# A graph network on one core: the second layer's gathers of sampled rows, without their wait for the mean matmuls of two groups back

## The reference, cut to what matters

```python
def _sage_mean(h, src, dst, W_self, W_neigh, b):
    agg = jax.ops.segment_sum(h[src], dst, num_segments=N_NODES)
    deg = jax.ops.segment_sum(jnp.ones((src.shape[0],), h.dtype), dst, num_segments=N_NODES)
    mean_neigh = agg / jnp.maximum(deg, 1.0)[:, None]
    return h @ W_self + mean_neigh @ W_neigh + b
h = relu(_sage_mean(x, src, dst, W_self0, W_neigh0, b0))
h = _sage_mean(h, src, dst, W_self1, W_neigh1, b1)
x = layernorm(x + h)
...
kj = k[src] + e                      # e = edge_attr @ We + be
alpha = einsum('ehd,ehd->eh', q[dst], kj) / sqrt(D)
attn = softmax of alpha over the edges of one dst
out = segment_sum((v[src] + e) * attn) + (x @ Wskip + bskip)
x = layernorm(x + elu(layernorm(out) @ Wlin + blin + x))
```

## Time and profile before

| | us |
|---|---|
| three runs | 1755.62, 1757.79, 1760.14 |
| median | 1757.79 |
| the profiled execution, own time | 1751.26 |
| its span, first to last instruction | 1749.4 |

### The profile page before, as it was taken

One profiled execution on the slowest core, in us unless ns is written; L12 is line 12 of the kernel. 1 busy time (PEld: TensorE's weight loads), 2 busy tenths in 40 slices (PEclk: granted clock), 3 DMA queues, 4 the chain that ended last, 5 costly groups with the idle time before them and its releaser, 6 DMA issues. The chain is left out here.

```text
span 1749.4 us, 34139 instructions
## 1 busy us (share of the span) xinstructions
PE 1524.3 (87%) x7745; PEld 1024.5 (59%) x7745; DVE 1327.1 (76%) x6197; ACT 1160.0 (66%) x3125; POOL 1041.2 (60%) x1038
## 2 busy tenths in 40 slices
PE   3599999999999998999688867999999999999872
PEld 2477777777777776777455543555555555455441
DVE  4799999999999996656366653777777777777762
ACT  0499999999999995333255541666666666666662
POOL 4688888868888773664455526455555555555320
PEclk9899999999999999999899988999999999999995
DMA  2356566544444442332388853233222232333210
GB/s 79 109 152 158 153 160 154 151 154 144 149 142 148 139 146 74 85 84 70 116 268 271 273 173 80 78 84 85 83 84 84 84 85 79 82 83 85 59 36 4
DMA packets 178820, 206.77 MB, mean 118 GB/s; under 512 B 36607, under 2 KB 104666, under 8 KB 178703
## 3 DMA queue, kind: packets, MB, share of 16 engines
q1 hardware_dynamic: 151502, 169.25, 31.5%
q0 software_dynamic: 27200, 36.26, 9.0%
HBM read 107.47 MB, written 106.49 MB: 122 GB/s over the span
## 5 line engine op out<-in xcount | busy, mean ns | idle before, releaser
L1307 POOL DMA_INDIRECT big<-x_tab,look x196 | 199.6, 1019 | 97.6 <-issue 56.1
L1324 POOL DMA_INDIRECT out_dram<-big,idx x98 | 99.2, 1013 | 259.1 <-DVE big L1640 126.3
L700 PE MATMUL pb<-MG_s,big 128*128 128x256 f32 x832 | 207.4, 392 | 41.5 <-issue 30.7
L700 PEld LDWEIGHTS pb<-MG_s,big 128*128 128x128 f32 x832 | 149.5, 189 | 143.7 <-issue 95.2
L725 ACT ACTIVATE big<-big 128x128 f32<-128x128 f32 x416 | 170.0, 481 | 0.0
L820 POOL TENSOR_TENSOR big<-big,cl 128x512 f32<-128x512 f32 x104 | 133.3, 1282 | 49.8 <-ACT big L749 40.5
L682 PE MATMUL pb<-C_s,big 128*128 128x128 f32 x832 | 161.6, 276 | 0.0
L683 PE MATMUL pb<-Ws1c_s,big 128*128 128x128 f32 x832 | 161.3, 276 | 0.0
L1057 POOL DMA_INDIRECT big<-h1e_tab,hidx x98 | 97.9, 999 | 103.9 <-PE pb L937 45.0
L334 POOL DMA_INDIRECT a_xs<-in_x_dram,idx x98 | 102.3, 1044 | 86.7 <-issue 47.6
L1408 PEld LDWEIGHTS pb<-Wg_s,big 128*128 128x128 f32 x784 | 95.8, 192 | 98.1 <-ACT big L1480 95.8
(11 more groups left out here) (345 smaller groups left out, 4015.1 us busy)
## 6 DMA issues: line engine op xcount, KB each, us to landing
big<-in_x_dram SPq DMA_DIRECT2D x104, 256.0 KB
x_tab<-big SPq DMA_DIRECT2D x98, 256.0 KB
out_dram<-big SPq DMA_DIRECT2D x98, 256.0 KB
ve_tab<-c_ve SPq DMA_DIRECT2D x98, 256.0 KB
c_ve<-ve_tab SPq DMA_DIRECT2D x98, 256.0 KB
h1e_tab<-a_rows SPq DMA_DIRECT2D x25, 256.0 KB
x_tab<-a_rows SPq DMA_DIRECT2D x25, 256.0 KB
big<-eT_tab SPq DMA_DIRECT2D x98, 64.0 KB
```

The lines of the kernel that those rows point to most:

```text
L700: t = pe.matmul(o, b_x1T[:, r * P:(r + 1) * P], MG_s[:], start=True, stop=True)
L1307: g.indirect_dma_start(out=o, out_offset=None, in_=x1_tab, in_offset=bass.IndirectOffsetOnAxis(ap=look[:, a, j:j + 1], axis=0), bounds_che ...
```

## The change

One line of `c_pool` is removed: POOL no longer waits for the mean matmuls of group `s - 2` before it issues the gathers of group `s`. The wait for the gathers of group `s - 4` stays, and so does PE's wait for the gathers of its group. No other engine's instructions change; the lines after L1054 have numbers lower by one.

```diff
         def c_pool(g):
             for s in range(NG):
                 landed_before(g, dma_c[s % 4], R * (s // 4))
-                after(g, "c_pmT", s - 2)
                 for r in range(min(R, NT - R * s)):
                     t = R * s + r
                     g.indirect_dma_start(out=h1s[:, t, :], out_offset=None, in_=h1e_tab,
```

## The result

The changed kernel takes 1864.01 us (median of 4 runs, 1863.36 to 1865.36), the kernel before 1756.84 (4 runs beside it, 1755.62 to 1760.14). The ratio is 1.0608, with a 95% interval of 1.059 to 1.0626: 107 us slower. The forecast was no change. The two profiled executions have spans of 1863.5 and 1749.4 us, 114.1 apart.

What follows compares the result with a forecast made beforehand. The prediction took a loop over PE, ACT and back to PE, 7.03 us a group without gathers, as the bound. Its terms summed 0 + 0 + 0 + 0 + 0 = 0, so 1757.8 us, range 1752.8 to 1763.

Steps and rivals of the forecast that it cites:

- The wait goes: POOL in stage c: loses 21 waits, 45.0 us of idle time, last gather starts at 974.5; saving on the path 0.
- The wait that stays: POOL's wait for the gathers of group s - 4: issued at least 15.6 us before, so cost 0.
- The start of stage d: Semaphores are cleared on POOL after the barrier in both versions: cost 0.
- DMA traffic packed closer: Stage c's gathers every 5.20 us a group instead of 7.03 load the DMA engines more: taken as 0, bounds 0 to +4.8 us.
- What bounds the kernel now: Stage c runs at 7.03 us a group, set by a loop PE, ACT, PE without gathers; POOL follows PE.
- DVE beside the gathers: DVE's L908 in stage c now meets POOL's gathers: costs neither anything, 0, with POOL off the path.
- The rivals: Four alternatives: late stores (slower, 7%), relieved last groups (faster, 4%), PE held by gathers (faster, 1%), no effect on POOL (1%).
- The edge-term stores land late: Denser gathers delay stage c's stores, so ACT and DVE wait for their buffer: +4.8 to +13.6 us, say 1767; chance 7%.
- what would show it: Right if POOL never waits on L937, last gather starts near 975, pace stays 7.03 and PE's gather wait stays 13 us.

Runs made afterwards that it cites:

- no_landing_wait_again: Changed kernel with eight gather semaphores instead of four, its wait now for group s - 8: 1856.95 us (kernel before 1746.75); in an earlier measurement 1727.99 (before 1727.33).
- changed_again: The changed kernel without any edit, measured again beside the kernel before (1746.75 us): 1857.19 us, ratio 1.0629.
- direct_loads_2: Changed kernel with plain DMAs of 128 consecutive rows from POOL in place of the gathers by index: 1759.49 us (kernel before 1754.36).

## Why the prediction was wrong

**"The wait goes", "The wait that stays", "The start of stage d": right.** POOL lost its 45.0 us of idle time, its last gather starts 35 us earlier, nothing on the path came from that. `no_landing_wait_again`, where the remaining wait never holds, takes 1856.95 us beside the 1857.19 of `changed_again`, so that wait costs nothing either.

**"DMA traffic packed closer": this step failed.** It was given 0 with bounds of 0 and +4.8 us, and cost 107. The bounds counted bytes and DMA time. What packing the gathers closer cost was the delay of TensorE's completion signals (108.0 us between the means of group 1 and group 3), and the bytes cost next to nothing: with `direct_loads_2` the DMA engines moved 315 GB/s, for 5 us over before. The bound's own size can be doubted too: it takes 256 KB for four gathers, while the earlier trace rows has 1.23 MB for the 81 gathers of that stretch, a quarter of that. In unaffected conditions the same term did come out at nothing: `no_landing_wait`, with gathers as dense, took 1727.99 us against 1727.33. The changed kernel itself was not measured there; the forecast would probably have held, by the luck of the conditions and not by its grounds.

The evidence that settled it for me was group 23, which kept its 7.04 us with no gather beside it. That group shows what fewer gathers do, and I carried it over to more. On a curve that is nearly flat from some 6.0 us per four gathers upwards and takes off below, a point on the flat side says nothing of the other.

**"What bounds the kernel now": right for before, and taken as fixed.** The loop PE, ACT, PE is 7.03 us long in before, and in after once the gathers are over (7.04); it took 7.0 to 7.2 in the unaffected `no_landing_wait` with dense gathers. I treated the handing over from PE to ACT as a property of the loop, where in affected conditions it depends on what POOL does at the time. The 2.12 us pause was read as idle time of an engine off the path, worth nothing. It kept the rate on the flat side.

**"DVE beside the gathers": right as to the cost.** L908 took 340 ns at the median in after (860 to 1000 us) against 342 before. Single ones took up to 501 ns, which the forecast of "neither of them anything" did not have; POOL's rate was as forecast.

**The rivals: none was the case.** All of them were about DMA landings or PE's share of the time; a late signal between engines was not among them. "The edge-term stores land late" had the right sign and asked for a wait on a DMA in front of L1140; the wait that came there is for PE (23.25 us, "remote").

**What the trace before held.** Stage a was the place to look, since of all the rows its gathers come nearest to the rate that the change would bring to stage c. Its groups took 6.3 us on average (5.7 to 8.0) and 5.7 in the last three, and its ACT and DVE waited on "remote" now and then. I used stage a for the duration of two instructions and not for its pace. A pace that is 0.6 us longer beside gathers, times the 14 groups, would have bounded the cost at +8 us from the nearest row, still far too low, but with the right sign, and with a wait on "remote" to look into.

**The wrong test in "what would show it".** The conditions on the gather's line and PE's wait for it were all met by a kernel 107 us slower. The condition on the pace was the one that could fail.

## What to carry to other kernels

A wait that paces an engine off the critical path can still be doing work: before taking it out, find a stretch of the same trace where that engine already runs at the rate it would have then, and compare the pace of the others there with a stretch without it. Here, in affected conditions, indexed gathers from GpSimd at less than some 6 us per four went with late hand-overs from TensorE; issuing them no faster than they are consumed cost the changed stage nothing in either kind. And when the same kernel comes out at 1727 and at 1757 us, look for the stage that differs before trusting a verdict from either.

## What the runs showed of the hardware that was not expected

- ACT and DVE can start 6 to 60 us after the (modelled) end of the matmul that they wait for while GpSimd issues indirect DMAs every 1.30 us; what waits for ACT or DVE in the same stretch starts within 0.1 us. The steepness: 7.0 to 8.5 us per group at 6.03 us per four gathers, up to 20 at 5.68, 39 to 78 at 5.21.
- Plain DMAs from GpSimd, one every 0.53 us at a DMA share of 0.95, did not do this.
- It appears in some conditions only, and not as a fixed trait of a chip: the chip of that number gave 1727.33 for before in one measurement and 1754.36 in a later one. All 12 affected traces hold 19,023 to 21,789 semaphore records, the 8 unaffected ones 36,307 to 36,368. What the conditions are, whether recording has a part in them, and by which path a gather holds up a signal of TensorE, stays open.
- GpSimd's sequencer ran up to twelve gathers, some 15 us, ahead of the engine (963.6 against 978.8 for the last), so that a wait placed in front of a gather acts much earlier than the gather's own start.
